# A graph network kernel: inputs of the convolution loaded per group of 1024 edges two groups ahead, four scatter row buffers, and the byte mask written by ScalarE as a sign

## The reference

```
h   = x @ W_in + b_in
Wij = (ssp(f_ij @ Wf1 + bf1) @ Wf2 + bf2) * edge_weight
agg = segment_sum(h[dst] * Wij, src)            # 103125 edges x 128
x   = layernorm(x + ssp(agg @ Wo1 + bo1) @ Wo2 + bo2)
```

## Time and profile before

| | us |
|---|---|
| median of 3 runs | 2540.95 (2538.02 to 2550.27) |
| the profiled execution | 2517.95 |
| its span | 2515.6 |
| PE busy | 1817.6 (72%) |
| DVE busy | 1425.8 (57%) |
| ACT busy | 721.6 (29%) |
| POOL busy | 1050.6 (42%) |
| convolution, first copy of h to first tail load | 194 to 1427 |
| counting stage | 1655 to 1973 |

### The profile page before, as it was taken

How to read it: one execution, slowest core, us unless ns; L and a number is a source line. 1 busy time by engine, 2 the same in 40 slices (tenths; PEclk the granted TensorE clock), 3 DMA queues, 4 the chain that set the end, 5 groups by cost and what they waited for, 6 DMA issues and landing times. The chain is left out here.

```text
span 2515.6 us, 36162 instructions
## 1 busy us (share of the span) xinstructions
PE 1817.6 (72%) x9002; PEld 1285.2 (51%) x9002; DVE 1425.8 (57%) x3122; ACT 721.6 (29%) x1166; POOL 1050.6 (42%) x863
## 2 busy tenths in 40 slices
PE   6269999799989799897998556366555567047775
PEld 4125555466656566564666456244444345036664
DVE  2694444445444454444445433569889432998884
ACT  1005544333333333333333200022322110033331
POOL 0106777666666666666666400047676200000000
PEclk9855555566775676767667787677678555568886
DMA  3103333444544444444444444013223200054440
GB/s 110 40 3 89 96 91 92 110 121 111 126 125 106 108 128 123 126 126 109 124 117 124 107 124 105 29 78 129 122 120 145 78 0 0 0 180 157 157 150 26
DMA packets 244631, 252.24 MB, mean 100 GB/s; under 512 B 49319, under 2 KB 206899, under 8 KB 241222
## 3 DMA queue, kind: packets, MB, share of 16 engines
q1 hardware_dynamic: 217070, 196.53, 27.8%
q0 software_dynamic: 25856, 53.42, 6.1%
q10 hardware_dynamic: 1624, 1.24, 0.2%
HBM read 150.63 MB, written 100.46 MB: 100 GB/s over the span
## 5 line engine op out<-in xcount | busy, mean ns | idle before, releaser
L1062 POOL DMA_INDIRECT edge_rows<-x_rows,pos_now x808 | 815.2, 1009 | 516.5 <-DVE x_rows L940 325.3
L830 PE MATMUL ps_wh<-wf,filt 128*128 128x128 f32 x1616 | 353.2, 388 | 2.9 <-DVE filt L929 2.5
L807 PE MATMUL ps_v<-f_t,wf 21*128 21x512 f32 x404 | 345.2, 948 | 12.8 <-DMA f_t<-in_f_t 12.8
L922 DVE TENSOR_SCALAR onehot_t<-dst_bc,base_p,win_off 126x512 bf16<-126x512 int16 x202 | 86.4, 428 | 446.3 <-DMA dst_bc<-dst 439.2
L830 PEld LDWEIGHTS ps_wh<-wf,filt 128*128 128x128 f32 x1616 | 316.2, 290 | 10.8 <-DVE filt L929 8.7
L839 PEld LDWEIGHTS ps_d<-back_one,back 128*128 128x128 f32 x1360 | 239.7, 268 | 151.8 <-issue 129.6
L1404 POOL TENSOR_SCALAR mask<-room 128x3150 uint8<-128x3150 f32 x25 | 219.2, 8780 | 173.9 <-ACT room L1493 173.9
L839 PE MATMUL ps_d<-back_one,back 128*128 128x128 f32 x1360 | 273.3, 371 | 0.0
L898 ACT ACTIVATE h_edge<-ps_wh 128x512 f32<-128x512 f32 x202 | 120.6, 597 | 512.0 <-PE ps_wh L830 509.7
L940 DVE SCALAR_TENSOR_TENSOR x_rows<-ps_wh,w_col,h_edge 128x128 f32<-128x128 f32 x808 | 226.7, 344 | 23.7 <-ACT h_edge L898 23.4
L1928 PE MATMUL ps_wh<-loan,wgt 128*126 128x129 f32 x1250 | 161.1, 294 | 77.3 <-DVE wgt L1879 77.2
(11 more groups left out here) (313 smaller groups left out, 2119.4 us busy)
## 6 DMA issues: line engine op xcount, KB each, us to landing
back<-edge_rows SPq DMA_DIRECT2D x75, 645.0 KB
c_tab<-room SPq DMA_DIRECT2D x25, 1575.0 KB, 5.3
c_in<-c_tab SPq DMA_DIRECT2D x25, 1575.0 KB, 6.5
dst_bc<-dst SPq DMA_DIRECT2D x202, 126.0 KB
edge_rows<-x_rows,pos_now POOLq DMA_INDIRECT x808
back<-edge_rows SPq DMA_DIRECT2D x25, 516.0 KB
f_t<-in_f_t SPq DMA_DIRECT2D x202, 40.0 KB
h_win<-h_table SPq DMA_DIRECT2D x202, 31.5 KB
```

The costliest lines, as they stand in the source:

```text
L807: nc.tensor.matmul(ps_v[:, j, :], wf1[:], f_t[:, j, :], start=True, stop=True).then_inc(v_done[j], 1)
L830: mm = nc.tensor.matmul(ps_wh[:, j, 0, q * D:(q + 1) * D], filt[:, j, q * P:(q + 1) * P], wf2[:], start=False, stop=True, skip_group_check ...
L1062: pool.indirect_dma_start(table[s], bass.IndirectOffsetOnAxis(pos_now[:, j, q:q + 1], 0), x_rows[:, j, q, :], None).then_inc(added[j][q], 16)
```

## The change

- The segments are cut at (0, 28, 56, 82, 101) and KS is (10, 10, 10, 7).
- f_t and dst_bc hold a group (1024 edges) each instead of a half, with two buffers by the parity u of the group; h_win is loaded once per group for both halves. All three are loaded for group i + 2 during step i. A group that spans more than one window of 42 nodes would load the others into h_more.
- SP's step: dst_bc and f_t of i + 2, then `back` of the next step's window, then the window load of i + 2. The wait for `back`'s buffer is as before.
- x_rows and pos_now get a buffer for each parity and half (4 in place of 2); the 4 scatters of a half share one semaphore.
- Where a segment has 28 groups, 25 or 24 windows of the one before are summed; the tail has 34 windows, 9 of ten tiles and 25 of seven.
- In the counting stage POOL does nothing; ACT, after copying a bank, writes the mask's bytes with a second instruction, Sign of the same bank, and c_mask goes.

```diff
-GS = (0, 27, 54, 81, NG)
+GS = (0, 28, 56, 82, NG)
-KS = (10, 10, 10, 8)
+KS = (10, 10, 10, 7)
...
-            f_t = tmp("f_t", [RBF + 1, 2, HALF])
-            dst_bc = tmp("dst_bc", [P, 2, HALF], I16)
+            f_t = tmp("f_t", [RBF + 1, 2, WG])
+            dst_bc = tmp("dst_bc", [P, 2, WG], I16)
             h_win = tmp("h_win", [3 * WN, 2, D], BF16)
+            h_more = tmp("h_more", [3 * WN, D], BF16)
-            x_rows = tmp("x_rows", [P, 2, TQ, RW])
-            pos_now = tmp("pos_now", [P, 2, TQ], I32)
+            x_rows = tmp("x_rows", [P, 2, 2, TQ, RW])
+            pos_now = tmp("pos_now", [P, 2, 2, TQ], I32)
...
-            added = [sems(f"added{j}_", TQ) for j in range(2)]
+            added = [sems(f"added{u}_", 2) for u in range(2)]
...
+                def load_dst(i, u):
+                    sp.dma_start(dst_bc[0:3 * WN, u, :],
+                                 dst16[bass.ds(i * WG, WG)].partition_broadcast(3 * WN)).then_inc(dst_in[u], 16)
+                def load_window(i, u):
+                    first = value(sp, ctrl[0:1, bass.ds(i, 1)], NP - WN)
+                    sp.dma_start(h_win[:, u, :], h_rows[window(first, 0), :]).then_inc(win_in[u], 16)
...
-                def half(i, j, last):
...
-                def step(i, new, old, last):
...
+                def step(i, h, u, new, old, nxt):
...
+                    if not is_last(i, 2):
+                        sp.wait_ge(onehot_done[1], i * n_win + n_win)
+                        stand_alone(sp)
+                        load_dst(i + 2, u)
+                        sp.wait_ge(v_done[1], i + 1)
+                        stand_alone(sp)
+                        load_f(i + 2, u)
+                    if nxt is not None:
+                        s, w = nxt[0:2]
                         if isinstance(w, int) and w == 0:
+                            all_added(sp, GS[s + 1])
+                        load_back(*nxt)
+                    if not is_last(i, 2):
+                        sp.wait_ge(win_used[1], i * n_win + n_win + 1)
+                        stand_alone(sp)
+                        load_window(i + 2, u)
...
-                    for q in range(TQ):
-                        need(dve, added[j][q], i * 16)
+                    need(dve, added[u][j], h * (TQ * 16))
...
-            @block.gpsimd
-            def _(pool):
-                for t in range(NB):
-                    pool.wait_ge(c_sb, (t + 1) * TGR)
-                    nc.gpsimd.tensor_scalar(mask[:, :, t * Q:(t + 1) * Q], stage[:, t % 2, :, :], 1.0, 0.0, ALU.min,
-                                            ALU.max).then_inc(c_mask, 1)
...
-                        act.wait_ge(c_mask, t - 1)
...
-                        nc.scalar.activation(cells(t % 2, g * GB * W), counted(count_bank(n)), ACT.Copy).then_inc(c_sb, 1)
+                        nc.scalar.activation(cells(t % 2, g * GB * W), counted(count_bank(n)), ACT.Copy)
+                        first = t * Q + g * GB * W
+                        nc.scalar.activation(mask[:, :, first:first + GB * W].rearrange("p h (b d) -> p b h d", d=W),
+                                             counted(count_bank(n)), ACT.Sign).then_inc(c_sb, 1)
```

More of the change, by code:

```diff
@@ L399, in _ @@
                 nc.vector.tensor_scalar(ctrl[:, NG:NG + 1], extra[:], 1.0, None, ALU.add)
+                nc.vector.tensor_copy(ctrl[:, NG + 1:NG + 2], extra[:])
                 link(nc.vector.tensor_scalar(base_row[:], lo_row[:], top[:, 0:1], None, ALU.min))
@@ L741, in load_back @@
                                  ).then_inc(back_in[u], 16)
-                def half(i, j, last):
[L744 to L753, removed]
-                        stand_alone(sp)
-                        load_f(i + 1, j)
@@ L757, in step @@
-                def step(i, new, old, last):
-                    if new is not None:
-                        s, w = new[0:2]
-                        if isinstance(w, int) and w == 0:
-                            for j in range(2):
-                                for q in range(TQ):
-                                    sp.wait_ge(added[j][q], GS[s + 1] * 16)
-                        load_back(*new)
-                    half(i, 0, last)
-                    half(i, 1, last)
+                def step(i, h, u, new, old, nxt):
+                    with sp.If(n_win > 1):
+                        first = value(sp, ctrl[0:1, bass.ds(i, 1)], NP - WN)
+                        for j in range(2):
+                            with sp.Fori(1, n_win) as w:
+                                sp.wait_ge(win_used[j], i * n_win + w + 1)
+                                sp.dma_start(h_more[:, :], h_rows[window(first, w), :]).then_inc(more_in, 16)
+                    if not is_last(i, 2):
+                        sp.wait_ge(onehot_done[1], i * n_win + n_win)
+                        stand_alone(sp)
+                        load_dst(i + 2, u)
[4 more added lines that the diff above has]
+                        s, w = nxt[0:2]
+                        if isinstance(w, int) and w == 0:
+                            all_added(sp, GS[s + 1])
[4 more added lines that the diff above has]
+                        load_window(i + 2, u)
@@ L768, in _ @@
                 sp.wait_ge(f_ones, 1)
[L769 to L770 removed]
+                for i in range(2):
+                    load_f(i, i)
+                    load_dst(i, i)
+                    load_window(i, i)
                 walk(sp, step)
                 sp.wait_ge(sum_b, STEADY)
[L773 to L775 removed]
+                all_added(sp, NG)
                 for n, (s, w) in enumerate(TAIL):
@@ L899, in copy_h, with step @@
                                          ACT.Copy).then_inc(h_copied[j], 1)
-                def step(i, new, old, last):
+                def step(i, h, u, new, old, nxt):
                     for j in range(2):
                         copy_h(i, j)
-                        if not last:
+                        if not is_last(i):
                             softplus(i + 1, j)
@@ L1052, in _, with step @@
             def _(pool):
-                def step(i, s):
+                def step(i, s, u):
                     for j in range(2):
```

154 lines of the change are left out of this document (80 added, 74 removed).

## The result

| | before | after |
|---|---|---|
| median of 4 runs, us | 2539.48 (2536.17 to 2550.27) | **3449.39** (3444.9 to 3455.3) |
| the profiled execution, its span | 2517.95, 2515.6 | 3444.9, 3443.1 |
| convolution | 194.5 to 1427.1: 1232.6 | 195.3 to 1242.3: 1047.0 |
| tail | 152.8 | 145.2 |
| extra pass | none | 1387.5 to 2570.1: 1182.6 |

The account below looks back on a forecast made before the run. It took PE, idle behind late loads, and POOL's scatters, near their limit, to bound the convolution. 2518 + 1157 (pass) - 120 (convolution) - 60 (count) + 5 (tail) = 3500, said as 3520 us for the median; range 3350 to 3750.

Parts of the forecast that it names:

- The windows don't fit: Summing: new cuts make fullest windows 1324 and 1298 of 1280, 948 of 896, so the extra pass runs once.
- rival 1: Summing: no second round, data or boundaries kinder than counted; 2366 us, faster than before; chance 0.04.
- The price of the pass: Extra pass: 100 serial windows, 75 at 12.14 us and 25 at 9.47, plus 10 for entering loops: +1157 us.
- head of SP's loop: Extra pass, each window: branch, value of bases and registers before the load, 1.3 us, taken from the nearest stretch.
- PE, to the addition: Extra pass, each window: PE's matmul halves, 4.24 us for 20 (ten tiles), 2.97 for 14 (seven).
- The convolution: Convolution: waits for dst_bc and h_win go, worth PE's idle 115 us; with smaller terms -120 us.
- POOL's floor: Convolution: 808 scatters of 1.262 us take at least 1020 us, bounding the gain at about -210 us.
- rival 4: Convolution: PE without gaps stays at 2.4 GHz and POOL bounds it all; 3430 us, chance 0.10.
- Rival 2: Convolution: second round runs and PE sits at 1.2 GHz through segments 1 to 3; 3726 us, chance 0.12.
- The count: Counting stage: without POOL's masks DVE runs undisturbed at 1.44 us a group, ACT's sign hidden: -60 us.
- rival 3: Counting stage: second round runs, and copy and sign load different ACT tables in turn; 3901 us, chance 0.03.
- The tail: Tail: 34 windows in place of 32, 9 at 5.24 us and 25 at 4.3, 155 against 149: +5 us.

Follow-up runs that it names:

- room for all: The kernel of after with KS = (11, 11, 10, 8), so every window fits and no extra pass runs: 2286.34 us on chip B, 2568.59 on A.

## Why the prediction was right, and where it was off

**The windows don't fit**: right, and **rival 1** with it out; this decides between slower and faster. The pass went over its 100 windows at the lines named; alone in before the cuts cost 1163 us.

**The price of the pass**: 1157 us said, 1182.6 measured. One window of ten tiles, from the timeline of after (columns as in the earlier trace rows):

```profile
1591.18 0.18 DVE L1065 SCALAR_TENSOR_TENSOR back_lo<-away,back 128x10 f32<-128x10 f32 x1 [5.50 <-DMA back<-edge_rows]
1591.39 1.49 DVE L1070 TENSOR_TENSOR tail_one<-back_lo,iota_f 128x1280 f32<-128x1280 f32 x1
...
1592.93 4.64 PE L904 MATMUL ps_d<-tail_one,back 128*128 128x128 f32 x20 [7.69 <-DVE tail_one L1070]
1597.72 0.29 DVE L1076 TENSOR_TENSOR agg_t<-ps_d,agg_t 128x128 f32 x1 [4.84 <-PE ps_d L904]
1599.16 0.38 SPq L817 DMA_DIRECT2D back<-edge_rows  x1
1603.53 0.17 DVE L1065 SCALAR_TENSOR_TENSOR back_lo<-away,back 128x10 f32<-128x10 f32 x1 [5.52 <-DMA back<-edge_rows]
```

| means, us | said, 10 tiles | 10 tiles (segment 0) | said, 7 | 7 tiles |
|---|---|---|---|---|
| head of SP's loop | 1.3 | 1.16 | 1.3 | 1.17 |
| load, to DVE | 4.55 | 4.49 | 3.57 | 3.77 |
| one-hots, to PE | 1.76 | 1.76 | 1.34 | 1.35 |
| PE, to the addition | 4.24 | 4.54 | 2.97 | 3.50 |
| addition | 0.29 | 0.29 | 0.29 | 0.29 |
| sum | 12.14 | 12.24 | 9.47 | 10.08 |

The next two segments take 12.54 and 12.34; in the first of them the head is 1.39 us. So 0.23 us in the mean for each of 75 windows and 0.61 for each of 25 (33 us), less some 7 of the 10 us for entering the loops, which took 3. The term that was low is PE's: 4.24 us came from one window of the tail, and the pass takes 4.54 to 4.59, at a mean clock of 0.59 to 0.61; for seven tiles the load, scaled from eight and ten, was low too. The head, for which there was no row, was bounded well by SP's issues.

**The convolution**: -120 us said, -186 measured. This is the term that was mis-sized: its worth was read from PE's idle time, "what they are worth is PE's idle 115 us, no more, if the clock's mean stays". What counted was POOL's. Before, POOL stood idle between scatters for 167 us more than in after; in after it runs from 197.3 to 1239.9 us with no pause over 0.32 us, 1042.6 us for its 808 scatters against the floor of 1020 (a scatter with its pause takes 1.30 us in segments 1 to 3, 1.27 in segment 0). PE's idle time hardly fell; the clock's mean rose and its busy time fell by 161 us, and why the clock rose no run here shows. The mechanism that set the time, POOL's floor, stood in the prediction only as a bound of -210 us and in rival 4. "Four row buffers let POOL lag by a group more; they don't make it faster" failed too: without them POOL runs out of rows, and they are worth 59 us. In segment 0 POOL took what was said, 284 us for its 28 groups, but the segment as PE sees it did not: its steps went at PE's 9.58 us a group, and the four buffers let POOL end its scatters 18 us after the segment's last step.

**Rival 4** (POOL the bound of the whole convolution, 3430 us, 0.10) is nearer to the result, 3449, than the forecast is, and its half about POOL is what the runs show: POOL's pauses are the same 0.3 us from end to end, and late loads of dst_bc cost nothing. Its other half, that PE stays at 2.4 GHz, did not come: the clock kept changing, at means of 0.78 to 0.85. The Trainium skill ("TensorE: Matmul & The Clock Gate", Part 1) says that activity releases the throttle. Segment 0 goes against it: PE is busy 267.97 of 268.12 us, and the matmuls take what they took at 0.50. Segments 1 to 3 don't bear it out either: the mean clock rose while PE was busy for 88% of the stretch before and 87% after. What keeps the clock low in segment 0 no run here shows. **Rival 2**, groups of 14.6 us at 1.2 GHz, is out: segments 1 to 3 need 776.5 / 73 = 10.6 us a group.

**The count**: -60 said, -64 measured. The sign, for which no row stood, by its instructions (ns shortest, median, longest):

```profile
L1510 ACT ACTIVATE room<-ps_v x88: 555/559/567, 2646.1 to 2895.2; 128x450 f32<-128x450 f32 x88
...
L1512 ACT ACTIVATE mask<-ps_v x88: 571/579/587, 2646.6 to 2895.6; 128x450 uint8<-128x450 f32 x88
```

0.58 us beside 0.54 said, with the copy 1.14 us of DVE's 1.44, hidden. No table load lies between the two, so **rival 3** is out. The Trainium skill ("ScalarE: Activation LUTs", Table sets: the hidden batching unit) says that cheap functions, copy among them, are in every set; it doesn't name sign there, and this trace shows that sign goes with copy.

**The tail**: +5 said, -8 measured. The first nine windows took 4.9 us each (5.24 said), the 25 of seven tiles 3.9 (4.3 said). The 5.24 came from the first two windows alone, while the seven of ten tiles took 4.80 each in before's own trace; the 4.3 was scaled from it.

The terms add up: +26 for the pass, -66 for the convolution, -13 for the tail, -4 for the count are -57 us against a sum of 3500, and the profiled execution took 3444.9. So nearly all of the miss is the convolution's 66; the pass and the tail with the count set each other off. The 20 us added for the median are the rest: this time it lay only 4.5 us above the profiled execution.

## What to carry to other kernels

A capacity that sits a few rows above its fullest case turns a retuned constant into a second code path: count the fullest case on the inputs before moving a boundary, and price the fallback, here 1.2 ms however few rows are over. Size a gain by the idle time of the engine that will be the bound when the waits are gone, here POOL and not the one that is busiest: buffers in front of it are worth what it would have idled. And a load need not come earlier by a whole group. That it should not stand in a queue behind another engine's late result is read from the waits (SP waited 326.6 us for sums before, 48.3 after); what the place in the queue alone costs is not measured.

## What was not expected of the hardware

**Chips differ.** The kernel of before takes 2539.48, 2541.22 and 2538.65 us on the first chip, B and C, and 2656.3 and 2681.14 us on A and D. POOL, which in after waits for rows no longer than 0.3 us at a time, pauses for 524 us between its scatters in room for all on A, against 247 on B. Room for all takes 2286.34 us on B and 2568.59 on A. Its convolution on A, segment 0 and the rest:

```profile
198.00:546.10 348.10, 275.49 (x841) 154.33 (x841) 130.18 (x446) 131.42 (x224) 210.31 (x218) 1.00 0.24 71
546.10:1531.20 985.10, 787.18 (x3591) 544.98 (x3591) 465.57 (x1495) 336.50 (x578) 594.89 (x591) 0.72 0.43 114
```

The longest waits in it:

```profile
ACT h_edge L924 <- remote: 730.7, 87, 12.3
DVE x_rows L967 <- ACT h_edge L924: 509.9, 83, 12.1
```

ACT waits 730.7 us for something that the trace doesn't name, 87 times, and there are moments when no engine starts anything, as in its timeline between 404.29 and 407.24 us:

```profile
404.29 0.96 POOL L1089 DMA_INDIRECT edge_rows<-x_rows,pos_now  x1 [0.31 <-issue]
407.24 0.00 SPq L757 DMA_DIRECT2D h_win<-h_table  x1
407.39 0.60 ACT L924 ACTIVATE h_edge<-ps_wh 128x512 f32<-128x512 f32 x1 [9.50 <-remote]
```

The extra pass takes 1176 us on A and 1183 on the first chip, DVE's part of the count 251 us on both: of the three only the convolution differs. My theory before the runs on chip B, that the code of the long steps arrives late, no run tests, and the cause stays open. A kernel whose waits are taken out gains less there (3.4% against 10.1%), so a gain has to be compared on one chip.
